# Moving the S visits of an attention and expert tower from eight to six visits ahead of T, with the first norms on POOL

## The reference

```
h = embeddings[x]                                   # 8 x 256 x 256
h = h + attention(layernorm(h))                     # 16 heads of 16, rotary q and k, softmax, w_proj
h = h + ffn(layernorm(h))                           # ffn(y) = y + y @ expert_w[argmax(gate_w @ y)].T
```

## Time and profile before

| what | value |
|---|---|
| median of 3 runs | 316.15 us (316.15 to 316.58) |
| the profiled execution's own time | 315.12 us |
| its span, first to last instruction | 313.3 us |
| PE busy | 282.4 us, 90% of the span |
| DVE busy | 246.3 us, 79% |
| ACT busy | 132.4 us, 42% |
| POOL busy | 86.4 us, 28% |
| mean granted TensorE clock | 0.998 |

### The profile page before, as it was taken

How to read it: one execution, slowest core, us unless ns; L and a number is a source line. 1 busy time by engine, 2 the same in 40 slices (tenths; PEclk the granted TensorE clock), 3 DMA queues, 4 the chain that set the end, 5 groups by cost and what they waited for, 6 DMA issues and landing times.

```text
span 313.3 us, 5632 instructions
## 1 busy us (share of the span) xinstructions
PE 282.4 (90%) x2073; PEld 201.9 (64%) x2073; DVE 246.3 (79%) x600; ACT 132.4 (42%) x271; POOL 86.4 (28%) x97
## 2 busy tenths in 40 slices
PE   2959988987889999989998999899999999999893
PEld 2738756555556776677766776676666666667582
DVE  8796977777997799797987798878898874566763
ACT  3155516646774533364435532463543454320100
POOL 5654005125786013431215031301210210210401
PEclk9999999999999999999999999999999999999999
DMA  3530232900940580029101840066010010000010
GB/s 115 195 129 7 74 129 58 152 9 11 146 61 9 94 115 2 2 83 146 21 0 45 143 62 4 33 110 96 2 37 3 2 36 2 4 29 5 0 36 33
DMA packets 10787, 17.55 MB, mean 56 GB/s; under 512 B 2008, under 2 KB 4867, under 8 KB 10632
## 3 DMA queue, kind: packets, MB, share of 16 engines
q1 hardware_dynamic: 9972, 16.62, 26.3%
q0 software_dynamic: 768, 0.55, 0.7%
q10 hardware_dynamic: 20, 0.02, 0.0%
HBM read 5.30 MB, written 2.10 MB: 24 GB/s over the span
## 4 chain that ended last, share of the span: by engine, by line
PE 48%; DVE 29%; issue 12%; POOL 6%; ACT 3%; DMA 1%; POOLq 0%; DVEq 0%
PE e_bank L467 14%; PE f_bank L467 7%; PE o_bank L629 7%; DVE neg_max L976 6%; DVE acc L1055 5%; PE t_pair L594 4%; POOL qk L386 3%; PE s_pair L467 2%; PE m_bank L641 2%; PE s_pair L564 2%; PE m_bank L467 2%; DVE xn L941 2%; POOL res L403 2%; DVE rope_b L963 1%; DVE rope_a L959 1%
## 5 line engine op out<-in xcount | busy, mean ns | idle before, releaser
L840 ACT ACTIVATE probs<-t_pair 128x512 f32<-128x512 f32 x128 | 69.7, 596 | 89.6 <-PE t_pair L594 89.0
L976 DVE TENSOR_REDUCE neg_max<-s_pair 128x2 f32<-128x512 f32 x128 | 82.0, 683 | 11.5 <-PE s_pair L564 11.4
L564 PE MATMUL s_pair<-stacks 48*128 48x256 f32 x256 | 48.2, 309 | 0.3 <-DVE neg_max L976 0.2
L594 PE MATMUL t_pair<-stacks 50*128 50x256 f32 x256 | 46.5, 308 | 1.6 <-DVE neg_max L976 1.1
L594 PEld LDWEIGHTS t_pair<-stacks 50*128 50x128 f32 x256 | 32.7, 185 | 23.4 <-issue 20.5
L467 PE MATMUL e_bank<-ew_h,y_h 128*128 128x512 f32 x92 | 40.3, 438 | 4.6 <-DVE acc L1051 2.7
L1055 DVE SCALAR_TENSOR_TENSOR acc<-e_bank,mask,acc 128x256 f32<-128x256 f32 x66 | 28.9, 479 | 11.2 <-PE e_bank L467 10.7
L386 POOL TENSOR_TENSOR qk<-rope_a,rope_b 128x512 f32<-128x512 f32 x16 | 20.9, 1307 | 60.4 <-DVE rope_b L963 60.4
L467 PE MATMUL e_bank<-ew_l,y_h 128*128 128x512 f32 x92 | 36.4, 395 | 0.0
L467 PE MATMUL e_bank<-ew_h,y_l 128*128 128x512 f32 x92 | 36.2, 394 | 0.0
L564 PEld LDWEIGHTS s_pair<-stacks 48*128 48x128 f32 x256 | 33.6, 185 | 3.0 <-DVE neg_max L976 1.3
(11 more groups left out here) (169 smaller groups left out, 552.9 us busy)
## 6 DMA issues: line engine op xcount, KB each, us to landing
stacks<-parts SPq DMA_DIRECT2D x36, 256.0 KB, 6.9
ew_raw<-in_expert_w SPq DMA_DIRECT2D x1, 2048.0 KB, 8.5
out<-res SPq DMA_DIRECT2D x8, 256.0 KB
stacks<-parts SPq DMA_DIRECT2D x12, 128.0 KB, 2.9
probs<-in_w_qkv SPq DMA_DIRECT2D x2, 384.0 KB, 3.5
stacks<-max_rows SPq DMA_DIRECT2D x30, 8.0 KB
h<-in_emb,ids POOLq DMA_INDIRECT x16, 5.3
probs<-in_w_proj SPq DMA_DIRECT2D x1, 256.0 KB
```

The source lines that it names most:

```text
L564: m = mm(s_pair[:, half, t * N:(t + 1) * N], stacks[b % STACKS][r:r + KS, pair, 0, t * P:(t + 1) * P], stacks[b % STACKS][r:r + KS, pair, ...
L594: m = mm(t_pair[:, half, c * N:(c + 1) * N], stacks[b % STACKS][r:r + KM, pair, 1, c * P:(c + 1) * P], stacks[b % STACKS][r:r + KM, pair, ...
L840: nc.scalar.activation(probs[:, (2 * v + half) % RING, :, :].rearrange("p c n -> p (c n)"), t_pair[:, half, :], ACT.Exp, scale=SCALE).then ...
L976: v.tensor_reduce(neg_max[:, k // 4, :, 4 * half + k % 4], s_pair[:, half, :].rearrange("p (t n) -> p t n", t=NT), AX.X, ALU.max, negate=T ...
```

## The change

S now runs six visits ahead of T instead of eight (`LAG = 2`, `scored`). In step b, visits 0 and 1 now carry S(b, 6) and S(b, 7) beside T(b, 0) and T(b, 1), and visits 2 to 7 carry S(b+1, 0) to S(b+1, 5) (T(0, 0) stands alone). The prologue does S(0, 0) to S(0, 6). The maxima of visits 4 to 7 are split in slot 3 instead of slot 0 of the next step and transposed in slot 5 instead of 3; those of visits 0 to 3 are split in slot 11 instead of 7 and transposed in slot 13 instead of 11 (9 for batches 1 and 2). The final multiply of the first layernorm of batches 2 to 7, and of the second of batches 0 to 6, moves from DVE to POOL (`f_scale`, `g_scale`). The expert weights are split in slots 1, 5, 9, 13 of steps 0 and 1 instead of all odd slots of step 1. The prologue's order changes on PE, DVE and POOL, and two `fill` calls go.

```
-        Z_ORDER = [(0, 0), (0, 1), (1, 0), (1, 1), (1, 2), (0, 2), (0, 3), (1, 3)]
+        Z_ORDER = [(t, q) for t in range(NT) for q in range(4)]
...
+        LAG = 2
+
+        def scored(b, v):
+
+            n = VISITS * (b + 1) + v - LAG
+            return n // VISITS, n % VISITS
...
+            def f_scale(b):
+                wait(pool, f_rstd, b + 1)
+                wait(pool, xt_ps, b)
+                for t in range(NT):
+                    g.tensor_scalar(xn[:, t, :], h0[:, b * NT + t, :], f_mv[:, t, 0:1], f_rs[:, t:t + 1],
+                                    ALU.subtract, ALU.mult).then_inc(f_scaled, 1)
+
+            def g_scale(b):
+                wait(pool, g_rstd, b + 1)
+                wait(pool, yt_ps, b)
+                for t in range(NT):
+                    g.tensor_scalar(yn[:, t, :], h1[:, t, :], g_mv[:, t, 0:1], g_rs[:, t:t + 1],
+                                    ALU.subtract, ALU.mult).then_inc(g_normed, 1)
...
-                    if s % 2 and b == 1:
-                        expert_weights([s // 2])
+                    if s % 4 == 1 and b < 2:
+                        expert_weights([4 * b + s // 4])
...
+            rotated_sum(0, 0)
+            rotated_sum(0, 1)
             gate_weights()
             proj_weights_low()
-            rotated_sum(0, 0)
-            rotated_sum(0, 1)
             rotated_sum(1, 0)
...
-                if g == 0 or g == 1 and maxima_slot(b + 1) == 9 or g == 2 and maxima_slot(b + 1) == 11:
+                if g in (0, 2):
                     outs_free(b, g)
...
-                    if here(b, 0) and s == 3:
+                    if here(b, 0) and s == 5:
                         max_transpose(b, 1)
-                    if here(b, 1) and s == maxima_slot(b + 1):
+                    if here(b, 1) and s == 13:
                         max_transpose(b + 1, 0)
...
             z_transpose(0)
-            fill(s_bank[0], 2)
+            project_qk(1, 1)
             z_transpose(1)
-            project_qk(1, 1)
-            visit(-1, 0)
+            visit(-1, 2)
             project_v(0)
-            visit(-1, 1)
+            visit(-1, 3)
...
-            project_qk(2, 0)
-            visit(-1, 5)
+            project_qk(2, 0, [0])
+            visit(-1, 7)
+            project_qk(2, 0, [1])
+            visit(-1, 8)
             project_qk(2, 1)
-            visit(-1, 6)
-            pe.wait_ge(roped, 2 * 2 * NT)
-            fill(t_bank[0], 3)
-            visit(-1, 7)
             pe.wait_ge(xl_ok, 3)
...
+            x_low(1)
             z_low(0)
-            x_low(1)
             z_again(1)
             z_low(1)
             rotate(1, 0)
-            f_norm_a(2)
             rotate(1, 1)
             maximum(0, 0)
-            f_norm_b(2)
+            f_norm_a(2)
             maximum(0, 1)
...
-            for k in range(4, VISITS):
+            for k in range(4, VISITS - 1):
                 maximum(0, k)
             steps(step)
```

More of the change, by code:

```diff
@@ L428, in step @@
                         f_rs_of(k)
+                        f_scale(k)
                     for k in batches(post, "stats", g_at):
                         g_rs_of(k)
+                        if not last(k):
+                            g_scale(k)
                     for k in batches(post, "g_norm", g_at):
@@ L460, in _, with product @@
             tr = nc.tensor.transpose
[L462 to L468, removed]
+            def product(o, xh, xl, wh, wl, parts=range(C)):
+                for c in parts:
+                    for n, (a, w) in enumerate(((xh, wh), (xl, wh), (xh, wl))):
+                        m = mm(o, a(c), w(c), start=(c == 0 and n == 0), stop=(c == C - 1 and n == 2))
                 return m
@@ L481, in x_transpose @@
                     wait(pe, qkl_ok, (b - 1) * NT)
-                wait(pe, f_normed, b * NT + NT)
+                if b < 2:
+                    wait(pe, f_normed, b * NT + NT)
+                else:
+                    wait(pe, f_scaled, (b - 2) * NT + NT)
                 for c in range(C):
@@ L500, in project_v, with project_qk @@
                 m.then_inc(v_ps, 1)
-            def project_qk(b, t):
-                if t == 0:
+            def project_qk(b, t, parts=range(C)):
+                if parts[0] > 0:
+                    pass
+                elif t == 0:
                     if b == 0:
@@ L599, in visit @@
             def visit(b, v):
+                k, w = (b, VISITS) if b == 0 and v == 0 else scored(b, v)
                 for half in range(2):
@@ L602, in visit @@
                         t_scores_wait(b, v, half)
-                    if here(b, 1):
-                        scores_wait(b + 1, v, 1 - half)
+                    if here(k, 0) and w < VISITS:
+                        scores_wait(k, w, 1 - half)
                     for i in range(NT):
@@ L607, in visit @@
                             t_scores_tile(b, v, half, i)
-                        if here(b, 1):
-                            scores_tile(b + 1, v, 1 - half, i)
+                        if here(k, 0) and w < VISITS:
+                            scores_tile(k, w, 1 - half, i)
             def outs_free(b, g):
@@ L1094, in step @@
                         f_norm_a(k)
-                    for k in batches(front, "norm", g_at):
-                        f_norm_b(k)
                     for k in batches(front, "x_low", g_at):
```

48 lines of the change are left out of this document (26 added, 22 removed).

## The result

The changed kernel takes **331.99 us** (median of 4 runs, 328.91 to 333.53), the kernel before 316.37 beside it (316.15 to 317.06): a ratio of 1.048, 95% interval 1.039 to 1.056. It is slower by 15.6 us where 5.4 less was forecast. The profiled execution took 333.53 us, with a span of 331.7.

A forecast was written before the change was run, and what follows sets the result against it. Waits bound the prologue and steps 0 and 1, PE the middle steps. Terms -4.1 - 3.5 - 0.7 + 2.9 = -5.4 took the profiled 315.12 to 309.7, a median of 310.7 us; range 308.4 to 312.6.

The forecast's parts named there:

- It reads one tensor, the addition two, so I take 0.45: Middle steps: POOL's yn instruction was taken to cost 0.45 us a tile, with bounds 0.25 and 0.64.
- The far end of the bounds: POOL's norm instruction might cost as much as the whole 512-element addition, 1.28 us a tile.
- The slower rival: y_transpose of batches 0 to 6 waits for POOL's late norms; 319.5 us at 1.28 us a tile; chance 0.09.
- The prologue: Up to the start of T(0, 0): it starts at 40.5 instead of 44.62, 4.1 us earlier.
- (a): Prologue: with x_low(1) ahead of z_low(0), PE's first product ends at 22.4 and its second near 25.1 instead of 28.9.
- (b): Prologue: ACT's copies, then DVE held by POOL, are late next; the first maximum starts at 27.5, 2.6 us earlier.
- (c): Prologue: seven visits of maxima with smaller gaps end at 39.8, so T(0, 0) starts at 40.5, 4.1 us earlier in all.
- Steps 0 and 1: Waits for maxima, max_rows, xn and o_l go or shrink: -3.0 us and -0.5, sum -3.5, bounds -1.5 and -5.0.
- Middle steps: Steps 2 to 4: yn ready earlier on POOL, half given back by the split; -0.25 us each, -0.7 in all.
- Steps 5 to 7: outputs waits 0.55 us for max_rows four times, plus later S and late yn: +2.9 us, bounds +1.5 and +4.5.
- B: The experiments' rival: the lag of six makes the loss, by later maxima; at least 325 us with norms on DVE; no chance given.
- C: The experiments' rival: the fill calls removed from the prologue let the clock fall; T(0, 0) at 44 or later; no chance given.

The follow-up runs named there:

- e11: The changed kernel with POOL's norm product cut to one operation and one scalar (subtraction of the mean left out); 321.96 us, ratio 1.018.
- e1: The changed kernel with all norm products (xn and yn) back on DVE; 319.33 us, ratio 1.009.
- e3: The changed kernel with filler matmuls ahead of x_transpose of batches 2 to 4 and of each y_transpose but the last; 326.74 us, ratio 1.031.
- e13: e9 with filler matmuls ahead of x_transpose(2) to (4) and of the 1.57 us wait in step 1; 312.82 us, ratio 0.990.
- e5: e1 with the split of the maxima moved to the end of its slot; 320.67 us, ratio 1.017.
- e7: The changed kernel with yn back on DVE, so only xn stays on POOL; 320.13 us, ratio 1.011.
- e4: e1 with the maxima transposed one slot earlier in steps 1, 5, 6 and 7; 315.83 us, ratio 0.999.
- e9: e1 with the late split in steps 2 to 4 only, earlier transposes in steps 1, 5, 6, and outputs(7, 0) behind the experts; 313.13 us, ratio 0.991.
- e10: The changed kernel with xn back on DVE, so only yn stays on POOL; 325.31 us, ratio 1.028.
- e14: e9 with the expert weights' copies and subtractions all in step 1 again; 313.54 us, ratio 0.993.
- e6: e4 and e5 together, plus six filler matmuls ahead of a wait for POOL's rotated sum in step 1; 320.40 us, ratio 1.016.
- e8: The kernel before with only the new order of the prologue, lag eight; 314.25 us, ratio 0.996.
- e12: e8 with filler matmuls where PE waits for maxima, at the prologue's last visit and step 0's first; 313.63 us, ratio 0.992.

## Why the prediction was wrong

**The step that failed** is "It reads one tensor, the addition two, so I take 0.45". POOL takes 1.23 us a tile. The far end of the bounds, 1.28, was right and was kept out of the range with 0.09. The nearest row priced an addition by its elements; this instruction, with two operations and two per-partition scalars, costs nearly as much for half of them. e11 shows that even one operation with one scalar takes 0.94. In the time this step is worth 12.7 us (e1). The Trainium skill (GPSIMD Engine Reference, "Elementwise — side-by-side cycle accounting") advises DVE for such work, and the runs agree with that advice; the estimate of 0.6 us a tile drawn from its addition was half of what was measured.

**It is not the only one.** With the norms back on DVE the forecast would still have failed: e1's profile is 4.2 us longer than before's, where 5.4 less was forecast. By parts it has -3.0 for -4.1 in the prologue, -0.1 for -3.5 in steps 0 and 1, +2.8 for -0.7 in steps 2 to 4 and +4.4 for +2.9 behind them. The two large misses are the waits of step 1 taken for gone and the split of the maxima ahead of two norms, both below.

**The slower rival had the mechanism and too small a price.** It gave 319.5 for 1.28 us a tile, by 1.26 us in each of seven steps. Measured with the lag's own order in place, the norms cost 12.7 us (e1). The waits for `yn` are 1.36 or 1.37 in the middle steps, and there the norms' move costs 0.3 to 0.9 (35.0, 34.8 and 34.7 for e1's 34.1, 34.3 and 34.4). What the rival missed is in the early and late steps: `xn`'s own waits (0.93, 1.06, 1.31), the queue behind `xn` and the weights in step 1 (3.40), and PE's clock, which e3 prices at 5.3 us. The prediction gave no wait a second price through the clock.

**The prologue.** (a) and (b) held: PE's first product ends at 22.2 and its second at 25.3, forecast 22.4 and 25.1, and the first maximum starts at 27.31, forecast 27.5. What ended last was not DVE's rotations, as (b) had it, but S behind ACT's copies, by 0.3 us:

```profile
27.31 1.29 DVE L1002 TENSOR_REDUCE neg_max<-s_pair 128x2 f32<-128x512 f32 x2 [0.29 <-PE s_pair L591]
```

(c) held by three quarters where the clock stayed up: T(0, 0) at 41.6 in e1, forecast 40.5, so 3.0 for 4.1. In the changed kernel the 3.0 were lost again between 33.3 and 40 us, to the lower clock: e3 has the same `xn` on POOL, fillers ahead of it and full clock, and is at 41.6.

**Steps 0 and 1.** Forecast -3.0 and -0.5. Without POOL's norms (e1) -2.0 and +1.9, with them -1.4 and +5.4. The terms named for step 0 (2.2 and 0.55) add to 2.75. In step 1 two of the waits that were to go are there in e1: 1.08 for `xn` (0.61 before) and 0.65 for `o_l` (0.66 before). The wait of `outputs` came as forecast (0.62 for 0.7), the one on the way of the maxima did not (0.2 in the whole run for 0.6). Beside them e1 has 3.4 us at the lower clock behind a wait of 1.57 for POOL's rotated sum; where fillers stood at that wait and at `xn`'s (e13) step 1 has 28.5, 0.7 above before. The kernel before has the same wait of 1.57 and kept its clock, so the prediction had no row that gave it a price.

**Middle steps.** Forecast -0.25 each; +1.2 to +2.0 measured. Of it 0.8 to 1.1 is there without POOL's norms (e1), and 0.8 of that is the split of the maxima in DVE's slots 3 and 11 (e5), which the prediction charged only for a collision with POOL and not for standing ahead of `norm0` and `g_norm`. The work that DVE lost (0.9 us less busy in step 3) did not show, since PE waited for POOL in its place. With only `xn` off DVE (e7) it is worth 0.5 to 0.7 a step against e1, no more than undoing the wait for `yn` that the split had made. A slip of the prediction's own changes little: transposes from 153.15 that take 0.66 end at 153.8, so the product could not start at 153.6.

**Steps 5 to 7.** Forecast +2.9 with four waits of 0.55 for `max_rows`; the profile has 0.55, 0.55, 0.56 and 0.76. The mechanism and size of these waits were right; e4 takes three of the four away and e9 the fourth. e1 gives +4.4 for the part without POOL's norms; in the changed kernel it is +9.8, with waits of 1.61 us for `yn` in steps 5 and 6 and a stretch at the lower clock behind each.

**The rivals of the study.** B holds for 3.1 of the 15.6 us net; in e1's profile it is 7.2 us behind T(0, 0) against 3.0 won ahead of it. It acts by the places of the split, the transposes and `outputs` and hardly by later maxima: e9 has the same lag, and its middle steps are back at 33.5 to 33.7. C is not refuted. e1, e5, e10 and e14 hold the upper level between 30 and 42 us without those fillers, e4, e6 and e9 do not, and it is worth about 1.2 us when it happens. Fillers help (e9 and e13, e8 and e12), but e12 shows that they do not decide it each time. What makes the clock fall in one execution and not in another stays open.

## What to carry to other kernels

Before an operation moves to another engine, price the operation itself there: if the trace has no row of that form, the far bound belongs in the range, and the question is at once who waits for its result. When a stage is moved by some slots, look at every small instruction that moves with it and at what stands behind it on its engine: two of 0.17 us ahead of a norm cost 0.4 to 0.5 us of PE, at two places in each step. Where PE has several waits close together, one of them can cost twice, by itself and by the clock after it, as behind waits of 0.93 to 3.40 us here; where it can't be removed, useless products ahead of it can be cheaper than idling. And before a mended change is called a gain, measure its parts alone: here the order of the prologue gives most of it.

## What the hardware showed that was not expected

- POOL's norm product on 128x256, two operations with a per-partition scalar each, takes 1.23 us, with one operation and scalar 0.94 (e11); its addition of 128x512 takes 1.28. Elements alone don't price it. DVE does two such tiles in 0.73.
- The granted clock of a kernel on one core differs between executions of the same program: the kernel before gave 314.57 to 314.94 us at 0.998 and 317.2 to 318.55 at 0.978 to 0.984, on one chip within one session. Kernels that differ by 1% need many runs, or fillers that hold the clock: e13's five runs lie within 0.4 us, e12's eight, with fillers too, within 2.1.
- The changed kernel's stretches at the lower clock lie behind waits of PE of 0.93 to 3.40 us, and waits of the same size elsewhere are followed by none (1.57 in the kernel before, 1.37 in the changed kernel's step 3).
